# A fused perceiver block on one core: the order of the last output projections and norms between head attention and the experts

## What is computed

```python
x = x + xattn(layernorm(x), ctx_1024, ...)   # 3 rounds of slot attention over 1601 context rows, with a GRU
x = x + attn(layernorm(x), Wqkv, bqkv, Wo, bo)     # 16 heads of 32 within each batch
x = x + ffn(layernorm(x), router_w, ..., shared_w2)   # 2 shared experts, and the best 2 of 8 routed ones
```

## Time and profile before

| | us |
|---|---|
| median of 3 runs | 900.07 (893.56 to 902.62) |
| the profiled execution's own time | 899.1 |
| its span | 897.4 |

### The profile page before, as it was taken

How to read it: one execution, slowest core, us unless ns; L and a number is a source line. 1 busy time by engine, 2 the same in 40 slices (tenths; PEclk the granted TensorE clock), 3 DMA queues, 4 the chain that set the end, 5 groups by cost and what they waited for, 6 DMA issues and landing times. The chain is left out here.

```text
span 897.4 us, 38761 instructions
## 1 busy us (share of the span) xinstructions
PE 766.7 (85%) x17710; PEld 640.4 (71%) x17710; DVE 588.1 (66%) x1131; ACT 366.2 (41%) x736; POOL 169.4 (19%) x441
## 2 busy tenths in 40 slices
PE   5697789998989999989998989798887897679994
PEld 2545689998988998978998889798664764324441
DVE  3987456876785876784876785746474777773224
ACT  3875415333525334434333431102175855342330
POOL 3020210311320311311211311102001025130003
PEclk9899889999999999999999999998988577869997
DMA  9986990374291454391463390701395600644414
GB/s 337 384 167 123 256 159 5 58 96 168 46 198 78 59 100 163 61 215 45 69 110 142 52 194 5 142 5 30 118 378 125 224 2 2 222 134 108 124 61 151
DMA packets 177887, 114.77 MB, mean 128 GB/s; under 512 B 146300, under 2 KB 156596, under 8 KB 174524
## 3 DMA queue, kind: packets, MB, share of 16 engines
q1 hardware_dynamic: 167084, 99.94, 45.9%
q10 hardware_dynamic: 8640, 6.56, 2.3%
q0 software_dynamic: 2000, 5.80, 2.2%
HBM read 61.94 MB, written 12.85 MB: 83 GB/s over the span
## 5 line engine op out<-in xcount | busy, mean ns | idle before, releaser
L1055 PE MATMUL banks<-qa,ctxT 128*128 128x64 f16 x3744 | 119.0, 195 | 14.6 <-issue 9.3
L1055 PEld LDWEIGHTS banks<-qa,ctxT 128*128 128x128 f16 x3744 | 115.8, 99 | 16.4 <-issue 10.1
L1006 PEld LDWEIGHTS banks<-wall,whhT 128*128 128x128 f16 x3456 | 109.7, 99 | 9.7 <-issue 4.3
L1006 PE MATMUL banks<-wall,whhT 128*128 128x64 f16 x3456 | 112.0, 194 | 3.1 <-issue 3.0
L1006 PE MATMUL banks<-qa,wall 128*128 128x64 f16 x3456 | 105.1, 193 | 1.4 <-issue 1.4
L1006 PEld LDWEIGHTS banks<-qa,wall 128*128 128x128 f16 x3456 | 102.6, 98 | 2.0 <-issue 1.6
L1074 PE MATMUL banks<-qa,wall 128*128 128x64 f16 (+1 forms) x1872 | 89.1, 195 | 9.7 <-issue 6.7
L1074 PEld LDWEIGHTS banks<-qa,wall 128*128 128x128 f16 (+1 forms) x1872 | 87.9, 100 | 10.9 <-issue 10.9
L1074 PE MATMUL banks<-wall 128*128 128x64 f16 (+1 forms) x936 | 87.9, 195 | 1.3 <-issue 1.3
L1074 PEld LDWEIGHTS banks<-wall 128*128 128x128 f16 (+1 forms) x936 | 84.4, 100 | 1.4 <-issue 1.4
L91 POOL TENSOR_TENSOR wall<-wall 128x64 f32<-128x64 f32 x24 | 12.5, 522 | 306.6 <-DVE wall L86 306.6
(11 more groups left out here) (289 smaller groups left out, 1496.2 us busy)
## 6 DMA issues: line engine op xcount, KB each, us to landing
wall<-in_ctx_dram SPq DMA_DIRECT2D x17, 1024.0 KB, 10.8
wall<-in_L_ffn_routed_w_dram SPq DMA_DIRECT2D x23, 512.0 KB, 7.4
unit<-in_ctx_dram SPq DMA_DIRECT2D x6, 1024.0 KB, 8.0
xg_scratch<-room SPq DMA_DIRECT2D x1, 3840.0 KB, 20.9
y_scratch<-room ACTq DMA_DIRECT2D x15, 256.0 KB, 2.1
ctxT<-in_L_xattn_gru_wih_dram SPq DMA_DIRECT2D x3, 1024.0 KB, 17.2
ctxT<-in_L_xattn_gru_whh_dram SPq DMA_DIRECT2D x1, 3072.0 KB, 25.6
ctxT<-in_L_attn_Wqkv_dram SPq DMA_DIRECT2D x12, 256.0 KB, 8.3
```

The source lines that it names most:

```text
L1006: mm = pe.matmul(dst[o], a, b, start=start, stop=True, skip_group_check=True)
L1055: mm = pe.matmul(score[n][:, t * K:(t + 1) * K], a, q, start=(k == 0), stop=(k == 3 * DC - 1), skip_group_check=True)
```

## The change

- In PE's loop `values(k)` stands ahead of `project`.
- In DVE's loop `add_y` stands behind `vals_low` and `wall_low`.
- The last projection, `project(3)`, writes bank 0 of `probT` in place of `yb`. It waits for ACT's last copies out of `probT` and no longer for `add_y(2)`, and stands right behind the turns of tiles 0 and 1, ahead of their router products.
- DVE's last `add_y` stands ahead of 9 `wall_low` chunks instead of behind them, and stores a guess too. GpSimd makes root and norm of tile 3 as it does those of the others; DVE's own at the head of the experts' block are gone.
- ACT copies tiles 0 and 1 ahead of two chunks, and DVE's `tile_low` of these tiles stands ahead of its two.
- In the experts' block PE turns tile 3 ahead of `up(0)`, ACT copies it first, and DVE's `tile_low` stands ahead of `gated(0)`.

```diff
+        def y_bank(t):
+            return yb[:] if t + 1 < RT else probT[:, 0, :]
...
-            for t in range(RT - 1):
+            for t in range(RT):
                 one = slice(t, t + 1)
                 pool.wait_ge(seeded, t + 1)
                 rsqrt_on(pool, st, var[:, one], rstd[:, one], tmp[:, one], more[:, one], root_out)
...
             vals_high(B - 1)
-            wall_high(act, e_all, IN_PROJECT + B - 3, IN_PROJECT + B - 1)
             for t in range(2):
                 tile_high(act, e_all, turn_bank(t), t)
-            wall_high(act, e_all, IN_PROJECT + B - 1, IN_HEADS)
+            wall_high(act, e_all, IN_PROJECT + B - 3, IN_HEADS)
...
-                dve.scalar_tensor_tensor(rows[:, t], yb[:], 1.0 / WS, rows[:, t], ALU.mult, ALU.add).then_inc(y_out, 1)
+                dve.scalar_tensor_tensor(rows[:, t], y_bank(t), 1.0 / WS, rows[:, t], ALU.mult, ALU.add).then_inc(y_out, 1)
...
-                if t + 1 < RT:
-                    dve.wait_ge(var_out, t + 1)
-                    root_seed(dve, st, var[:, t:t + 1], rstd[:, t:t + 1], seeded)
+                dve.wait_ge(var_out, t + 1)
+                root_seed(dve, st, var[:, t:t + 1], rstd[:, t:t + 1], seeded)
...
-                if k >= 4 and k % 2 == 0:
-                    add_y((k - 4) // 2)
                 if k >= 1:
                     vals_low(k - 1)
                 if k >= 3:
                     wall_low(dve, e_all, IN_PROJECT + k - 3, IN_PROJECT + k - 2)
+                if k >= 4 and k % 2 == 0:
+                    add_y((k - 4) // 2)
             vals_low(B - 1)
             add_y(RT - 2)
-            wall_low(dve, e_all, IN_PROJECT + B - 3, IN_PROJECT + B - 1)
             for t in range(2):
                 tile_low(dve, e_all, turn_bank(t), t)
+            wall_low(dve, e_all, IN_PROJECT + B - 3, IN_PROJECT + B - 1)
+            add_y(RT - 1)
             wall_low(dve, e_all, IN_PROJECT + B - 1, IN_HEADS)
-            add_y(RT - 1)
             tile_low(dve, e_all, turn_bank(2), 2)
...
             def project(t):
                 pe.wait_ge(vals_lo, 2 * (t + 1))
-                if t >= 1:
+                if t + 1 == RT:
+                    pe.wait_ge(pT_out, 2 * B)
+                elif t >= 1:
                     pe.wait_ge(y_out, t)
...
-                        mm = pe.matmul(yb[:], a, b, start=(n == 0), stop=(n == 3 * DC - 1))
+                        mm = pe.matmul(y_bank(t), a, b, start=(n == 0), stop=(n == 3 * DC - 1))
...
+                values(k)
                 if k >= 3 and k % 2 == 1:
                     project((k - 3) // 2)
-                values(k)
             pe.wait_ge(shifted, B)
             for t in range(2):
                 turn_tile(pe, c, e_all, turn_bank(t), t)
+            project(RT - 1)
             for t in range(2):
                 router_products(pe, e_all, t)
-            project(RT - 1)
             turn_tile(pe, c, e_all, turn_bank(2), 2)
             router_products(pe, e_all, 2)
...
+            tile_high(act, e, yb[:, LAST], LAST)
             for t in range(LAST):
                 rows_high(t)
...
                 if b == 0:
-                    tile_high(act, e, yb[:, LAST], LAST)
                     rows_high(LAST)
...
-            var, rstd, tmp = (e.root[:, j, LAST:] for j in range(3))
-            rsqrt(dve, st, var, rstd, tmp)
-            dve.tensor_scalar(e.xn[:, LAST], rows[:, LAST].rearrange("p (c r) -> p c r", c=DC), e.mv[:, LAST, 0:1], rstd,
-                              ALU.subtract, ALU.mult).then_inc(e.x_ready, 1)
+            tile_low(dve, e, yb[:, LAST], LAST)
             gated(0)
-            tile_low(dve, e, yb[:, LAST], LAST)
...
             for b in range(NALL + 2):
+                if b == 0:
+                    turn_tile(pe, c, e, yb[:, LAST], LAST)
                 if b < NALL:
                     up(b)
                 if b == 0:
-                    turn_tile(pe, c, e, yb[:, LAST], LAST)
                     router_products(pe, e, LAST).then_inc(routed, 1)
```

## The result

| | before | changed |
|---|---|---|
| median, us | 901.17 (893.56 to 902.62, 4 runs) | 907.25 (906.24 to 911.71, 4 runs) |
| span of the profiled execution | 897.4 | 905.8 |

The ratio is 1.0076, with a 95% interval of 1.0045 to 1.0107: slower by 0.76%, clear of no change. The median is within the range 900.5 to 911 and 1.45 us above the forecast 905.8. The forecast's ratio was 1.0064 of its own base, 900.07.

The account below looks back on a forecast made before the run. Whatever moves the start of `choose()`, set by the last engine to end head attention, moves the end. GpSimd's 5.4 us plus 0.3 in the experts' block, 5.7, added to the median 900.07 gave 905.8 us; range 900.5 to 911.

Parts of the forecast that it names:

- `add_y` in the loop: DVE's loop: `norm(5)` starts 1.35 us later, `norm(7)` another 1.5; PE waits for both, so all behind is 2.9 us later.
- `values(7)` ahead of `project(2)`: PE's last loop round: the reorder gains nothing; `add_y(2)` starts at 754.8 instead of 751.92, still 2.9 us late.
- `project(3)` in its own bank: Tail of head attention: DVE's wait for it is gone or at most 1.7 us, but this buys DVE no time.
- The end on GpSimd: End of head attention: GpSimd's fourth norm ends last at 771.0, 5.4 us behind the earlier 765.60.
- The experts' block: Head of the block: 0.3 us added in all; `up(1)` 1 us earlier, unawaited; nothing changes from `choose()` on.
- Sum: Whole kernel: 5.4 us at the end of head attention plus 0.3 in the experts' block, 5.7 us slower.
- The signs that the prediction had named: Norms right behind a guess, GpSimd last, block at 771 to 772, first routed `up` near 806, later ones 2.59 us.
- GpSimd not last: End of head attention: DVE ends the block instead, 3.4 plus 0.3 us, total 903.8; chance 0.12.
- The loop hides `add_y`: DVE's loop: ACT's exponentials turn out later anyway, so 2.9 us fall away, total 902.9; chance 0.06.
- Full clock: PE kept at 2.4 GHz in loop and experts' head: 9.3 us less, net gain 3.6, total 896.5; chance 0.06.
- A lower clock for longer: PE at 1.2 GHz for `project(2)`, `up(0)`, turn and values: 3.2 us more, total 909.0; chance 0.16.

Follow-up runs that it names:

- e1: The changed kernel with DVE's loop `add_y` ahead of `vals_low` and the chunk again; ratio to the kernel before 1.0047.
- e2: The changed kernel with tile 3 turned and copied behind `up(0)` again in the experts' block; ratio to the kernel before 1.0045.
- e5: The changed kernel with PE's `values(k)` behind `project` again; ratio to the kernel before 1.0061.
- f4: f3 with `values(7)` ahead of `project(2)` in the last round alone; ratio to the kernel before 0.9966.
- f5: f4 with two more chunks cut at the end of head attention instead of in the experts' block; ratio to the kernel before 0.9964.
- f1: The kernel before with only `project(3)` early in its own bank and the tail order that goes with it; ratio to the kernel before 0.9982.
- f2: The kernel before with only six chunks moved from DVE's tail into its idle times in the loop; ratio to the kernel before 0.9985.
- e3: The changed kernel with tile 3's root and norm on DVE again and the old experts' order; ratio to the kernel before 1.0035.
- e4: The changed kernel with all eleven chunks of the tail ahead of `add_y(3)`; ratio to the kernel before 1.0109.
- f3: The kernel before with both f1's own bank for `project(3)` and f2's six moved chunks; ratio to the kernel before 0.9968.

## Why the prediction was right, and where not

*`add_y` in the loop* (1.35 and 1.5 us). Right. From the end of the exponentials `norm(5)` starts 1.23 us late; from `turn_probs(6)` to `norm(7)` it is 3.66 us against 2.33. e1 takes it back. What had no term is the clock between the two norms, 0.7 us here and 1.2 in e2 against e1. On the axis of the first exponential `norm(7)` is 2.5 us late, not 2.9, since PE also had 0.8 us of luck with the clock around `project(0)`.

*`values(7)` ahead of `project(2)`* (nothing gained). Right in its order, wrong in its length. Taking out `project(2)` itself, it is 3.0 to 3.3 us from `turn_probs(7)` to `add_y(2)` in all twelve profiles, whichever order: values first pushes the projection back by 1.2 to 1.5 us and hides the 1.5 us of values, copies and `vals_low` behind it (e5). The prediction named only the first of these, and had the second within the 751.92 that it compared with. What it mis-sized is the projection, 3.39 us as before where 4.24 was measured, so that `add_y(2)` came 3.3 us late and not 2.9. And the order does act on that length: it is 0.7 us shorter with values first where the clock rises at the same mark (f4, f5 against f1, f2).

*`project(3)` in its own bank* (buys DVE no time). Right, and f1 shows it alone: 5.6 us earlier for `add_y(3)`, nothing for the block.

*The end on GpSimd* (5.4 us). Right in what ends the block, and it starts 5.3 us later. That the two numbers meet is in part chance. From `add_y(2)` to the block it is 15.9 us against 14.0, 1.9 more, where the forecast has 2.5 more; `add_y(2)` made up for it by being later than forecast. The norms took 5.7 and 7.9 us, where I had 6.6 and 7.6. PE and DVE alone would have ended it 3.3 us later (771.72 against 765.60, less 2.86), where I had 3.4. e3 takes GpSimd out and gets 2.0 us back; e4 shows that 3.0 of the fourth norm's 7.9 us are the chunks.

*The experts' block* (0.3 to `choose()`, nothing behind it). The first part was right: 7.29 against 7.22 us. The second was wrong: "`up(1)` comes 1 us earlier, which nobody waits for". Nobody does, but PE is idle 1.65 us longer ahead of the counting products, they run at 1.2 GHz, and DVE waits 1.6 us more for them. e2 takes it away. The Trainium skill (TensorE: Matmul & The Clock Gate, What's actually happening) told that an idle PE falls back to 1.2 GHz; I had applied it to the waits I saw and not to the one the edit makes.

*Sum.* From the first exponential to the end of the span the change cost 5.5 us, the forecast was 5.7: 5.3 to the block, 0.1 to `choose()`, 1.6 for the counting, and 1.4 given back behind the first routed `up`, 0.65 by the clock there and 0.8 by the last transfer of routed rows to `y_scratch` (3.16 us against 3.94). The prediction had neither the 1.6 nor the 1.4. The 5.3 to the block, mark by mark and rounded: 0.8 less ahead of `turn_probs(4)`, 1.2 more up to `norm(5)`, 0.7 up to `turn_probs(6)`, 1.3 up to `norm(7)`, 0.9 by `project(2)` up to `add_y(2)`, 1.9 up to the block. So the sum is close partly since misses of both signs cancel. The other 2.9 us between the two spans lie ahead of head attention. The signs that the prediction had named are there: on the axis of the kernel before, the block starts at 771.2 and the first routed `up` at 807.4, it still waits for a chunk, and the later routed `up`s take 2.59 us in both kernels.

*The rivals.* GpSimd not last: no, by the rows at the block's start. The loop hides `add_y`: no. Full clock: no; of its terms `up(0)` and the first routed `up` were only 0.2 and 0.3 us shorter than before, and both projections longer (its 1.3 us for `project(1)` should have been 1.65, 4.24 less 2.59). `project(3)`, which it doesn't list, ran at 2.4 GHz, where nothing waited. A lower clock for longer: in part, 0.85 us at `project(2)`, and in two places that I hadn't listed, 0.7 us between `norm(5)` and `turn_probs(6)` and the 1.6 of the counting.

## What to carry to other kernels

A product that comes earlier is worth nothing if the engine that uses it is still busy with its own list. Here DVE's list set the end, and `project(3)` 5.6 us earlier bought nothing (f1). Read the user's whole list up to the next point where all engines meet, and move work that fills waits (here the weight chunks) into idle times that are there, not behind the thing waited for (f3).

When an engine gets one more item, as GpSimd did, count the item ahead of it in its queue, and what runs on the engine that slows it.

Where an edit makes PE's wait longer, look at what PE does next: both in the loop and at the counting products the work behind the longer wait had a lower granted clock, and it was on the path.

And before a difference of 1 us is put down to an edit, look for a second profile with the same instructions in that stretch. e2, e3 and e4 showed that the changed kernel's slow `project(2)` wasn't the edit's.

## What was unexpected of the hardware

- The counting products (16 small float32 matmuls) took 2.0 us after a wait of 1.17 us and 3.6 us after one of 2.82: the granted clock fell to 0.5 within the wait. In e1, after a wait of 2.81 us, the first group still ran as fast as before (0.41 us) and the last as slowly as in the changed kernel (1.85).
- Ten GpSimd instructions on one column took 0.19 to 0.23 us each alone and up to 0.70 beside DVE's chunks: the longest are about as long as a chunk (0.68).
- A wait of 2.6 us instead of 1.4 ahead of `turn_probs(5)` went with a mean granted clock of 0.59 to 0.60 instead of 0.70 to 0.71 over the 12 us behind it, in five profiles against seven.
- Without any edit ahead of it, the same loop reached `norm(7)` at marks up to 1.1 us apart from one profile to the next, by the instants at which the clock changed.
